# A graph network of four layers: edge masks made in layer 0, layer 2's scores added by TensorE in PSUM, x2 added by GpSimd, the last softmax over five steps

## The reference, cut to what is computed

```python
x = layernorm(x + L0(x))   # score = exp(clip(k[src] . q[dst])); mean of v[src] weighted by it
x = layernorm(x + L1(x))   # z = (1+eps)*x + sum of x[src]; two products with relu; layernorm; relu
x = layernorm(x + L2(x))   # e = a_src[src] + a_dst[dst], 8 heads, also for an edge of each node to itself
                           # e = max(e, 0.2*e); alpha = softmax of e over the edges of one target
                           # y = sum(alpha * h[src]) + bias + x; layernorm(y) * ln_w + ln_b
x = layernorm(x + L3(x))   # alpha = softmax over one target's edges of q[dst] . (k[src] + edge_attr @ We)
                           # y = sum(alpha * (v[src] + edge_attr @ We)) + x @ Ws + bs
```

## Time and profile before

| | us |
|---|---|
| median of three runs | 5241.77 (5236.48 to 5249.33) |
| the profiled execution | 5255.12 |
| its span | 5253.4 |

### The profile page before, as it was taken

One profiled execution on the slowest core, in us unless ns is written; L12 is line 12 of the kernel. 1 busy time (PEld: TensorE's weight loads), 2 busy tenths in 40 slices (PEclk: granted clock), 3 DMA queues, 4 the chain that ended last, 5 costly groups with the idle time before them and its releaser, 6 DMA issues. The chain is left out here.

```text
span 5253.4 us, 92503 instructions
## 1 busy us (share of the span) xinstructions
PE 4759.6 (91%) x22307; PEld 3673.2 (70%) x22356; DVE 3938.6 (75%) x13675; ACT 2788.8 (53%) x6264; POOL 2227.9 (42%) x2267
## 2 busy tenths in 40 slices
PE   5999997789999999998888888888789999788888
PEld 3666654478888888886677777777556665677776
DVE  5777779978888888886499999999945555566666
ACT  1878875545555555554366565666511111455555
POOL 4555532265555555553455555555265554000000
PEclk8999995589999999999799999999899999899999
DMA  5777769834444444443466666666455554767675
GB/s 142 221 223 224 222 206 306 275 105 131 131 134 131 131 134 132 130 133 117 137 185 193 184 194 184 192 194 183 131 169 163 164 163 139 213 206 217 203 219 159
DMA packets 864002, 921.99 MB, mean 176 GB/s; under 512 B 104707, under 2 KB 820026, under 8 KB 863660
## 3 DMA queue, kind: packets, MB, share of 16 engines
q1 hardware_dynamic: 447188, 420.18, 27.7%
q10 hardware_dynamic: 333688, 318.57, 17.9%
q0 software_dynamic: 82784, 179.41, 11.7%
HBM read 632.08 MB, written 337.88 MB: 185 GB/s over the span
## 5 line engine op out<-in xcount | busy, mean ns | idle before, releaser
L1165 POOL DMA_INDIRECT nodes_near_rows<-hh_d,source_row x392 | 396.8, 1012 | 592.0 <-DVE nodes_weighted L1338 515.8
L565 POOL DMA_INDIRECT layer_xg<-in_x,edge_rows x392 | 386.5, 986 | 339.9 <-PE layer_t_ps L602 220.6
L836 POOL DMA_INDIRECT nodes_near_rows<-x_d,nodes_cur x392 | 426.4, 1088 | 235.8 <-POOL nodes_cur L831 171.2
L1481 POOL DMA_INDIRECT edges_xg<-x_d,edge_rows x392 | 371.4, 947 | 258.6 <-PE edges_x_ps L1507 176.2
L466 ACT ACTIVATE nodes_x<-nodes_outer_rows,nodes_outer_shift,nodes_outer_rstd 128x256 f32<-128x256 f32 x784 | 426.0, 594 | 12.6 <-issue 7.1
L1723 PE MATMUL nodes_agg<-w_s,nodes_xT 128*128 128x256 f32 x1568 | 414.4, 388 | 1.3 <-ACT nodes_xT L1740 1.3
L844 POOL TENSOR_TENSOR nodes_xb<-nodes_xin,row_L_gnn_b 128x512 f32<-128x512 f32 x196 | 248.2, 1266 | 380.2 <-DVE nodes_inner_rows L870 380.0
L949 PE MATMUL nodes_h_ps<-w_h,nodes_x2T 128*128 128x272 f32 x1568 | 392.2, 393 | 6.7 <-ACT nodes_x2T L1026 6.7
L1536 ACT ACTIVATE edges_xT<-edges_x_ps 128x512 f32<-128x512 f32 x196 | 117.1, 597 | 526.0 <-PE edges_x_ps L1507 526.0
L959 PE MATMUL nodes_hid_ps<-nodes_zT,w_a 128*128 128x256 f32 x1568 | 372.3, 380 | 0.7 <-ACT nodes_zT L1035 0.7
L635 PE MATMUL layer_agg<-layer_msg,layer_hot 128*128 128x264 f32 x784 | 313.1, 539 | 65.7 <-issue 65.7
(11 more groups left out here) (218 smaller groups left out, 12589.0 us busy)
## 6 DMA issues: line engine op xcount, KB each, us to landing
nodes_xin<-x_d SPq DMA_DIRECT2D x588, 256.0 KB, 3.0
x_d<-nodes_x ACTq DMA_DIRECT2D x392, 256.0 KB, 2.4
layer_msg<-msg_d SPq DMA_DIRECT2D x392, 132.0 KB, 3.7
hh_d<-nodes_hh ACTq DMA_DIRECT2D x196, 264.0 KB, 2.4
nodes_msg<-msg_d SPq DMA_DIRECT2D x392, 132.0 KB, 3.5
x_d<-layer_y ACTq DMA_DIRECT2D x196, 256.0 KB, 3.9
nodes_hin<-hh_d SPq DMA_DIRECT2D x196, 256.0 KB, 3.9
out<-nodes_y ACTq DMA_DIRECT2D x195, 256.0 KB, 3.2
```

What stands on the lines that cost most here:

```text
L565: gp.indirect_dma_start(out=xg[:, c % 8, k, :], out_offset=None, in_=x, in_offset=bass.IndirectOffsetOnAxis(ap=edge_rows[:, c, k:k + 1], a ...
L836: gp.indirect_dma_start(out=near_rows[:, r, h, :], out_offset=None, in_=x1_d, in_offset=bass.IndirectOffsetOnAxis(ap=cur[:, r, h:h + 1], a ...
L1165: gp.indirect_dma_start(out=near_rows[:, u % NR, h, :], out_offset=None, in_=hh_d, in_offset=bass.IndirectOffsetOnAxis(ap=source_row[:, 2 ...
L1481: gp.indirect_dma_start(out=xg[:, c % 8, k, :], out_offset=None, in_=x3_d, in_offset=bass.IndirectOffsetOnAxis(ap=edge_rows[:, c, k:k + 1] ...
```

## The change

- Masks: all 25 groups' lists are loaded at the start of `layer0` on SyncE's queue (8 large and 8 small DMAs), and VectorE makes `go_on` and `fresh` (bf16) for one group in each of 25 steps there. `nodes2` and `nodes3` load no pairs and make no masks. `BIG` becomes a power of two.
- `nodes1`: GpSimd gets a second addition at 11, x2 + `ln_b` into `x2b`; what is stored as x2 is this, at 13 rather than 11.
- `nodes2`: ScalarE copies the source parts of the scores, TensorE adds the parts by products with the identity into `score_ps`, at 11; ScalarE makes a fifth of it, VectorE takes the maximum; the softmax's tiles stay in PSUM, and its instructions stand singly between others of steps 12 and 13 (`mark` without a wait, `settle` ahead of the next). x2 is no longer summed by TensorE: GpSimd adds it to `own` at 16. GpSimd's addition of `ln_b` and its clearing of `near_rows` (now VectorE's, one slot a step) go. The attributes' turning and product come twelve steps later (`LATER`). `hin`, `xin`, `weighted` and `own` have 5, 9, 4 and 4 buffers rather than 6, 6, 3 and 3.
- `nodes3`: the softmax is spread over steps 10 to 14, turned at 15, used at 16; all later work comes four steps later; `msg` has 24 buffers rather than 16, `weighted` 6 rather than 4; SyncE's program is written out, with `xin` at 11.
- `prepare`: `ln_b` is taken off layer 2's bias (one instruction).

```diff
+                sp.wait_ge(lists_out, 16)
+                for h in range(H):
+                    sp.dma_start(pairs[h * 2 * GU:(h + 1) * 2 * GU, 0:WHOLE, :],
+                                 windows[0:WHOLE * 2 * GU, :].rearrange("(g w) x -> w g x", w=2 * GU)).then_inc(pairs_in, 16)
+                    sp.dma_start(pairs[h * REST:(h + 1) * REST, WHOLE, :], windows[WHOLE * 2 * GU:TILES, :]).then_inc(pairs_in, 16)
...
+                def masks(of, g):
+
+                    if g == 0:
+                        ve.wait_ge(pairs_in, 2 * H * 16)
+                    target = pairs[of, g, :].rearrange("p (e w) -> p e w", w=2)
+                    link(nc.vector.tensor_tensor(go_on[of, g, 1:P], target[:, 1:P, 1], target[:, 0:P - 1, 1], ALU.is_equal))
+                    nc.vector.tensor_scalar(fresh[of, g, :], go_on[of, g, :], BIG, -BIG, ALU.mult, ALU.add)
...
+                    if MASKS <= s < MASKS + WHOLE:
+                        masks(slice(0, P), s - MASKS)
+                    if s == MASKS + WHOLE:
+                        masks(slice(0, REST * H), WHOLE)
...
-                run_steps(gp, UNITS, 2, body)
+                    u = at(11)
+                    if u:
+                        gp.wait_ge(outer["normed"], num(u) + 1)
+                        if had(u, 4):
+                            gp.wait_ge(x2_out[ring(u, 4)], turn(u, 4) * 16)
+                        gp.tensor_tensor(x2b[:, ring(u, 4), :, :], x2[:, ring(u, 4), :, :], both(rows["L2_gnn_ln_b"]), ALU.add)\
+                          .then_inc(x2_biased, 1)
+                run_steps(gp, UNITS, 11, body)
...
-                            act.wait_ge(x2_out[ring(u, 4)], turn(u, 4) * 16)
+                            act.wait_ge(x2_biased, num(u) - 3)
...
-                        act.dma_start(unit_rows(x2_d, u), x2[:, ring(u, 4), :, :]).then_inc(x2_out[ring(u, 4)], 16)
...
+                        act.wait_ge(x2_biased, num(u) + 1)
+                        act.dma_start(unit_rows(x2_d, u), x2b[:, ring(u, 4), :, :]).then_inc(x2_out[ring(u, 4)], 16)
...
+    def top_run(g, n, run, of_edges):
+
+        return nc.vector.tensor_tensor_scan(run, fresh[0:n, g, 0:P], of_edges, -BIG, ALU.add, ALU.max)
+
+    def back_over(g, n, to, run):
+
+        return nc.vector.tensor_tensor_scan(to[:, ::-1], fresh[0:n, g, 1:P + 1][:, ::-1], run[:, ::-1], -BIG, ALU.add, ALU.max)
+
+    def sum_run(g, n, run, of_edges):
+
...
+        NR, HR, XR, WR, HOT, LATER = 16, 5, 9, 4, 18, 12
...
+                        gp.wait_ge(own_done, u + 1)
+                        gp.wait_ge(x_in[u % XR], u // XR * 16 + 16)
+                        gp.tensor_tensor(own[:, u % WR, :, :], own[:, u % WR, :, :], xin[:, u % XR, :, :], ALU.add).then_inc(based, 1)
...
+                    g = at(11)
+                    if g is not None and g % GU == 0:
+                        g //= GU
+                        n = of_group(g) * H
+                        pe.wait_ge(near_all, g + 1)
+                        pe.wait_ge(e_copied, GU * g + n // (2 * H))
+                        if g:
+                            pe.wait_ge(share_ready, g)
+                        for k, first in enumerate((near_score[:, 0:n], att_edge[:, g % 2, 0, 0:n])):
+                            nc.tensor.matmul(score_ps[0:n, k * P:(k + 1) * P], first, ident[:, :], start=True, stop=False)
+                            last = nc.tensor.matmul(score_ps[0:n, k * P:(k + 1) * P], att_edge[:, g % 2, 1, 0:n], ident[:, :], start=False, stop=True)
+                        last.then_inc(score_summed, 1)
+                    u, e, k = at(2), at(2 + LATER), s - 2
...
-                        pe.wait_ge(own_done, u + 1)
+                        pe.wait_ge(based, u + 1)
...
-                            nc.tensor.matmul(cols, ident[:, :], xin[:, u % HR, h, :], start=False, stop=False)
...
+                    g = tops
+                    if g is not None:
+                        n = of_group(g) * H
+                        ve.wait_ge(fifth_ready, g + 1)
+                        mark(nc.vector.tensor_tensor(score_ps[0:n, 0:2 * P], fifth[0:n, :, :].rearrange("p k e -> p (k e)"),
+                                                     score_ps[0:n, 0:2 * P], ALU.max))
+                    g = shares
+                    if g is not None:
+                        n = of_group(g) * H
+                        ve.wait_ge(exped, g + 1)
+                        mark(sum_run(g, n, score_ps[0:n, 2 * P:3 * P], score_ps[0:n, 0:P]))
...
+                        mark(top_run(g, n, score_ps[0:n, 2 * P:3 * P], score_ps[0:n, 0:P]))
...
+                        mark(back_over(g, n, top[0:n, :], score_ps[0:n, 2 * P:3 * P]))
...
+                        mark(back_over(g, n, total[0:n, :], score_ps[0:n, 2 * P:3 * P]))
...
+                        both_scores = score_ps[0:n, 0:2 * P].rearrange("p (k e) -> p k e", k=2)
+                        nc.vector.tensor_tensor(both_scores, both_scores, spread(top, n), ALU.subtract).then_inc(less_ready, 1)
...
+                        nc.vector.tensor_tensor(share[0:n, 0, :], score_ps[0:n, 0:P], total[0:n, :], ALU.mult)
+                        mark(nc.vector.tensor_tensor(score_ps[0:n, P:2 * P], score_ps[0:n, P:2 * P], total[0:n, :], ALU.mult))
...
+                        nc.vector.scalar_tensor_tensor(share[0:n, 1, :], score_ps[0:n, P:2 * P], -1.0, fresh[0:n, g, 0:P],
+                                                       ALU.add, ALU.mult).then_inc(share_ready, 1)
...
+                            nc.scalar.activation(head_columns(near_score, n).rearrange("p (u w) h -> p u w h", w=2),
+                                                 near_rows[:, u0 % NR:u0 % NR + n // 2, :, D:D + H], ACT.Copy).then_inc(near_all, 1)
...
+                        nc.scalar.activation(fifth[0:n, :, :].rearrange("p k e -> p (k e)"), score_ps[0:n, 0:2 * P], ACT.Copy, scale=0.2)\
+                            .then_inc(fifth_ready, 1)
...
-        MR, XR = 16, 8
+        MR, XR, WR = 24, 8, 6
...
+                    g = group(10)
+                    if g is not None:
+                        n = of_group(g) * H
+                        ve.wait_ge(score_turned, g + 1)
+                        mark(top_run(g, n, run[0:n, :], score_ps[0:n, 0:P]))
+                    g = group(12)
+                    if g is not None:
+                        n = of_group(g) * H
+                        ve.wait_ge(exped, g + 1)
+                        mark(sum_run(g, n, run[0:n, :], grown[0:n, :]))
+                    g = group(13)
+                    if g is not None:
+                        n = of_group(g) * H
+                        settle()
+                        mark(nc.vector.reciprocal(total[0:n, :], total[0:n, :]))
+                    g = group(14)
+                    if g is not None:
+                        n = of_group(g) * H
+                        settle()
+                        if g:
+                            ve.wait_ge(share_turned, g)
+                        nc.vector.tensor_tensor(share[0:n, :], grown[0:n, :], total[0:n, :], ALU.mult).then_inc(share_ready, 1)
```

More of the change, by code:

```diff
@@ L1062, in head_columns @@
         return t[:, 0:n * H].rearrange("p (h w) -> p w h", h=H)
-    def softmax_buffers(sb, sem):
-        t = {"pairs": sb("pairs", [P, 2, P, 2], I32), "target": sb("target", [P, P]), "keep": sb("keep", [P, P + 1]),
-             "join": sb("join", [P, P + 1]), "first": sb("first", [P, P]), "run": sb("run", [P, P]), "top": sb("top", [P, P]),
-             "less": sb("less", [P, 2, P]), "grown": sb("grown", [P, 2, P]), "total": sb("total", [P, P]),
-             "share": sb("share", [P, 2, P])}
-        for name in ("chain", "edges_set", "pairs_in0", "pairs_in1", "cast", "less_ready", "exped", "share_ready", "back"):
-            t[name] = sem("sm_" + name)
-        return t
@@ L1279, in _ @@
             def _(ve):
-                link = chained(ve, sm["chain"])
-                set_edges(sm)
-                ve.wait_ge(zeroed, 1)
+                mark, settle = marked(ve, chain)
                 def body(s, at):
+                    if s < NR:
+                        nc.vector.memset(near_rows[:, s, :, :], 0.0).then_inc(zeroed, 1)
+                    tops, shares = (g // GU if g is not None and g % GU == 0 else None for g in (at(12), at(13)))
                     u = at(19)
@@ L1323, in body @@
                         norm_measure(ve, outer, (None, 8, u))
+                    g = tops
+                    if g is not None:
+                        n = of_group(g) * H
+                        settle()
+                        mark(nc.vector.tensor_tensor(top[0:n, :], top[0:n, :], score_ps[0:n, P:2 * P], ALU.max))
+                    g = shares
+                    if g is not None:
+                        n = of_group(g) * H
+                        settle()
+                        mark(nc.vector.tensor_tensor(total[0:n, :], total[0:n, :], score_ps[0:n, P:2 * P], ALU.add))
                     u = at(20)
@@ L1587, in nodes3 @@
```

(41 more changed lines are left out.)

473 lines of the change are left out of this document (218 added, 255 removed).

## The result

The changed kernel takes **5017.74 us** (median, 5013.86 to 5020.77), the kernel before 5245.53 beside it; the ratio is **0.9568, 95% interval 0.9551 to 0.9584**. The profiled execution takes 5013.86 us with a span of 5012.1.

The account below looks back on a forecast made before the run. In `nodes2` TensorE bounds ordinary steps and VectorE group steps, in `nodes3` the softmax's chain costs; -150 - 36 (`nodes2`) - 84 (`nodes3`) + 8 (`nodes1`) + 3 (`layer0`) = -259: 4996 profiled, 4983 median, range 4905 to 5085 us.

Parts of the forecast that it names:

- The group work: `nodes2`, VectorE: masks, scores, tops and shares together fall from 7.97 to 4.1 us a period.
- the two named waits: `nodes2`, VectorE: about 0.8 us around the shares for ScalarE's table changes, 2.1 for its late root, each period.
- the 5.9: `nodes2`: us of each period before the change counted as waits, the largest visible one 2.75 for ScalarE's root.
- the 2.6 that the prediction let go: `nodes2`: waiting expected to vanish per period, 3.3 of 5.9 us staying, because TensorE's ordinary step gets shorter.
- the 1.49 of L1390: `nodes2`, shares: us a group saved on VectorE's product, 1.91 against 0.42, once its operands lie in PSUM.
- plus 0.5: `nodes3`: us added to TensorE's period because turning the shares overwrites the old group's, whose `weighted` lies in the same step.
- the 2.39: `nodes3`: us of TensorE's stall before the turning of the shares in the old period, blamed on the softmax's serial chain.
- The third: `nodes1`, shared port: one block plus partial ones bring the step to 7.3 to 8.2 us, 5030 to 5210; chance 0.12.
- fourth rivals: `nodes1`: both GpSimd additions block VectorE's two-tile instructions and gathers run late; slower, 5290 at step 8.6; chance 0.04.
- The upper end of 14: `layer0`: most that the list loads ahead of the first windows might cost, in us; 3 was taken.
- The sign named for being wrong: `layer0`: a first window after 120 us would show the forecast wrong.
- The first rival: `nodes2` waits survive, period 47.4, 60 us less gain, half of `nodes3`'s stall stays: 5045 to 5080; chance 0.20.

Follow-up runs that it names:

- the four kernels above: Kernel before without GpSimd's `ln_b` addition, without TensorE's x2 product, with first-group masks only, and with all three: `nodes2` 1236.7, 1342.7, 1329.3, 1177.0 us.

## Why the prediction was right, and where it wasn't

1. **Which stages.** Right: 259 of the 260 us gained lie in `nodes2` and `nodes3` by the table, and `nodes1` kept its pace.
2. **`nodes2`'s period.** Forecast 44.8, measured 43.85. The group work came out as said (3.8 for 4.1) and, in the group shown, the two named waits too: 0.8 expected before the shares and 0.81 seen, 2.1 at the root and 1.79 seen. Over the middle of the stage they are 0.85 and 1.28 a group, so the root's was set too high. The number of periods was 24, not 23, and the period before 51.10 on the mean. The 4.1 is 1.65 + 2.45 and has no place for the maximum, which was priced at 0.35; it came out because the four other instructions of the tops took 1.16 rather than 1.65, which was luck.
3. **What freed the waits.** Wrong, and only luck kept it from harming the sum: "the pace of TensorE in ordinary steps (5.31 against 4.68) was much of the 5.9 and goes". Taking TensorE's product out of the kernel before freed 0.15 us a period. Of the group's 5.9 us that the prediction calls waits, 3.33 are waits (2.75 and 0.58 for the outer root) and 2.38 are `hot`, which takes 2.22 and 1.08 us where it takes 0.46. Over the middle of the stage `hot` beyond its 86 us fell from 2.1 to 0.5 us a group and the outer root's wait from 2.9 to 1.3, while 0.85 for the exponential came new: 2.4 in all, about the 2.6 that the prediction let go for another reason. Leaving out GpSimd's addition is worth 4.27 of the 7.25, the first term by far, and the prediction priced only one of its places in the kernel before, the 1.49 of L1390. The changed kernel still has one such addition in `nodes2`, but there it costs 0.37. TensorE's pace counts once VectorE is no longer blocked: 1.8 in the kernel before, 3.8 in the changed one.
4. **`nodes2`'s start.** 30 for 36. Right in cause, since none of the four kernels above changes it (68.8 in each); the first product came 38.9 us after the stage's start, forecast 33.
5. **`nodes3`.** The step that failed: "plus 0.5 since `weighted` of the old group, which the turning overwrites, lies in the same step". It is 2.07 (28.31 - 26.24). The prediction put the 2.39 before the turning down to the softmax's chain, while the earlier trace rows name their releaser, `weighted` L1653, the last reader of the old shares. The spreading took the 1.15 at the scores; the rest went when the shares were turned into another bank than the group before. The mean period went from 30.78 to 28.39, 57.4 us in 24; the stage's start and end cost 7.4 of that, forecast 7.
6. **`nodes1`.** Right in mechanism and place, and the slack of 1.34 for a block of 1.27 was as tight as said: VectorE is busy 990 of 1000 us. 3.9 for 8. The third and fourth rivals didn't come, but the fourth's mechanism is there, and one more such addition costs 178.
7. **`layer0`.** The row used, 0.49 us for each issue, is of an idle queue. The upper end of 14 was the right value; I took 3. The sign named for being wrong, a first window after 120 us, missed by half a microsecond if it is read as TensorE's first sum (119.5).
8. **The Trainium skill's rule** on who interferes with whom ("SBUF — State Buffer", section "Who interferes with whom") was used by half. For VectorE instructions that read two tiles of SBUF the traces agree: the product of L1390 went from 1.73 us on the mean to 0.425 without GpSimd's addition, and a pair of L955 grew from 0.84 to 3.76. The same section of the Trainium skill says that a VectorE instruction in a two-port performance mode contends with GpSimd too, and that `tensor_scalar` can enter one; that half would have named `hot`, which reads one wide tile and a column of `target_rel`. The traces agree as far as they go: `hot` takes up to 2.05 us where it takes 0.28, and in the kernel before an f32 `tensor_scalar` over 392 columns takes 0.364 us (L703) where a `tensor_tensor` takes 0.568 (L705). No run shows by itself which mode `hot` ran in.
9. **Sums.** TensorE's period in `nodes2` is 8 x 4.45 + 0.6 = 36.2, not 36.8, and stays below VectorE's 41.5. The first rival's time is 4983 + 60 + 20 to 40, that is 5063 to 5083, not 5045 to 5080. Neither changes the forecast.

## To carry to other kernels

Before pricing an engine's step, take each line's shortest and longest duration: a spread like 0.28 to 2.05 us on one shape was blocking here, since it went when GpSimd's addition was left out, and it belongs in the sum at every place, not only where it is first seen. A part's gain depends on what else holds the loop: the same product on TensorE was worth 0.15 us a period while VectorE was blocked, some 1.8 once it was not, and 3.8 in the changed kernel, so leave out parts singly and together. And a releaser that the trace names before a stall (here the last reader of a PSUM tile) is to be believed before the longer chain that ends near it: laying each group's scores and shares in one bank, and the groups in two banks by turns, gave 52 us on top of the 50 from spreading the chain over five steps.

## What the hardware showed that I had not expected

- A VectorE instruction can lose more than the recorded length of the GpSimd addition that it meets: `hot` took 2.05 us at most against a shortest of 0.26, while the addition takes 1.27. A gather lies right before the addition, and what the first half microsecond is due to stays open. A pair of L955 lost 2.9 us to two additions that followed each other, 2.5 us long.
- GpSimd seems to be held as well: in `nodes1` the new addition takes 1.39 us at the median and 1.61 at most, the old one, of the same shape, 1.28 and 1.29.
- Sixteen list loads held SyncE's queue for 23.4 us, 1.5 each and single ones up to 8.4, where eight such loads took 3.9 in `nodes3`.
- Two chips differ by 0.9% on the same kernel (5249 and 5296 us), and not evenly: by the changed kernel's variants `edges3` differs by 2%, the start of `nodes2` by 8 us, `nodes1` not at all.
